# Moving the softmax denominators of a unit to one score bank, and the rows of their reciprocals to GpSimd

## The reference

```python
qkv = (tokens @ w_proj + b_proj).reshape(B, N, NUM_HEADS, 3 * HEAD_DIM)
q, k, v = jnp.split(qkv, 3, axis=-1)
attn = jnp.einsum('bihd,bjhd->bijh', q, k) * SCALE
attn = jax.nn.softmax(attn, axis=2)
res = jnp.einsum('bijh,bjhd->bihd', attn, v).reshape(B, N, NUM_HEADS * HEAD_DIM)
out = res @ w_out + b_out + tokens
```

## Time and profile before

| | before |
|---|---|
| median of 3 runs | 3090.85 us (3090.58 to 3091.7) |
| the profiled execution, its own time | 3092.63 us |
| its span in the profile | 3090.9 us |
| TensorE busy | 2674.5 us, 87% |
| VectorE busy | 2051.6 us, 66% |
| ScalarE busy | 1279.2 us, 41% |
| GpSimd busy | 635.7 us, 21% |
| granted TensorE clock, mean | 0.937 |

### The profile page before, as it was taken

One profiled execution on the slowest core, in us unless ns is written; L12 is line 12 of the kernel. 1 busy time (PEld: TensorE's weight loads), 2 busy tenths in 40 slices (PEclk: granted clock), 3 DMA queues, 4 the chain that ended last, 5 costly groups with the idle time before them and its releaser, 6 DMA issues.

```text
span 3090.9 us, 44860 instructions
## 1 busy us (share of the span) xinstructions
PE 2674.5 (87%) x15742; PEld 1889.2 (61%) x15742; DVE 2051.6 (66%) x2355; ACT 1279.2 (41%) x1860; POOL 635.7 (21%) x405
## 2 busy tenths in 40 slices
PE   6889979899798897988879888899888899888993
PEld 4457755577556775567755677457764477645772
DVE  4666667666676676666667566765677666766666
ACT  2553326433264333643336333463334533255334
POOL 0520116102160022500225002340024200252011
PEclk8999989999899998999999999999999999999996
DMA  6100050000500005000040001400022000410016
GB/s 150 32 25 1 1 130 2 25 1 14 117 1 25 1 14 117 2 24 1 21 110 1 24 1 36 95 12 14 1 66 66 25 1 1 95 37 25 1 55 245
DMA packets 46397, 124.71 MB, mean 40 GB/s; under 512 B 9792, under 2 KB 21312, under 8 KB 42560
## 3 DMA queue, kind: packets, MB, share of 16 engines
q1 hardware_dynamic: 46144, 121.41, 14.4%
HBM read 43.01 MB, written 23.86 MB: 22 GB/s over the span
## 4 chain that ended last, share of the span: by engine, by line
PE 74%; DVE 8%; issue 5%; ACT 5%; SPq 4%; DMA 3%; DVEq 0%; ACTq 0%
PE tile L1356 24%; PE pv L1356 10%; PE pv L1474 8%; PE tile L1436 7%; PE tile L1464 6%; PE tile L1623 4%; PE tile L1498 4%; SPq L522 3%; DMA stack<-qk_r 2%; PE pv L1464 2%; PE tile L1645 2%; PE tile L1753 1%; PE tile L1672 1%; PE tile L1523 1%; PE tile L1506 1%
## 5 line engine op out<-in xcount | busy, mean ns | idle before, releaser
L965 DVE TENSOR_REDUCE small<-tile 128x1 f32<-128x1024 f32 x512 | 599.1, 1218 | 169.8 <-PE tile L1436 169.8
L744 ACT ACTIVATE p<-tile 128x512 f32<-128x512 f32 (+1 forms) x640 | 410.2, 688 | 234.0 <-PE tile L1464 233.9
L1436 PE MATMUL tile<-stack 96*128 96x512 f32 x1024 | 348.8, 437 | 83.0 <-ACT stack L752 49.1
L1356 PE MATMUL tile<-qk_r 128*128 128x512 f32 x1536 | 377.9, 395 | 0.0
L653 POOL TENSOR_TENSOR row_sum<-act 128x256 f32<-128x256 f32 x32 | 42.1, 1334 | 1501.4 <-DVE act L1191 1501.4
L623 POOL TENSOR_TENSOR acc<-acc,p 128x1024 f32<-128x1024 f32 x144 | 339.4, 2385 | 0.0
L1436 PEld LDWEIGHTS tile<-stack 96*128 96x128 f32 x1024 | 177.8, 196 | 255.5 <-issue 118.1
L1356 PEld LDWEIGHTS tile<-qk_r 128*128 128x128 f32 x1536 | 287.1, 188 | 66.4 <-issue 7.7
L1196 DVE TENSOR_TENSOR pl<-p,ph 128x1024 fp32r<-128x1024 f32 x128 | 158.2, 1236 | 238.0 <-ACT p L838 238.0
L1464 PE MATMUL tile<-stack 112*128 112x512 f32 x768 | 271.2, 421 | 16.1 <-DVE rec L1013 9.2
L1474 PE MATMUL pv<-p,v 128*32 128x512 f32 x2048 | 271.8, 604 | 1.4 <-ACT p L744 1.4
(11 more groups left out here) (285 smaller groups left out, 4546.6 us busy)
## 6 DMA issues: line engine op xcount, KB each, us to landing
stack<-qk_r SPq DMA_DIRECT2D x192, 256.0 KB, 5.0
x_in<-in_x_dram SPq DMA_DIRECT2D x9, 1024.0 KB, 7.6
act<-in_x_dram SPq DMA_DIRECT2D x8, 1024.0 KB, 8.0
x_scratch<-act SPq DMA_DIRECT2D x7, 1024.0 KB, 3.9
z_scratch<-zbuf SPq DMA_DIRECT2D x7, 1024.0 KB, 5.3
stack<-ones SPq DMA_DIRECT2D x8, 512.0 KB, 7.6
w3f<-w3f_scratch SPq DMA_DIRECT2D x8, 512.0 KB, 3.3
fin_rest<-z_scratch SPq DMA_DIRECT2D x3, 1024.0 KB, 12.7
```

The lines of the kernel that those rows point to most:

```text
L744: sc.activation(p0[:, jt % DEPTH, pair, first:first + len(heads) * HALF], tile_wait(b, "st0", *u, jt, k), ACT.Exp, scale=float(D) ** -0.5) ...
L965: ve.tensor_reduce(maxima[:, h * NT + it:h * NT + it + 1], t[:], X, ALU.max).then_inc(vector_done, vector.one("max0", g, h, it))
L1356: ins = mm(out, lhs[a][kt_], rhs[c][kt_], start=first and kt_ == 0 and m == 0, stop=last and kt_ == n - 1 and m == 2)
L1436: ins = mm(o[:, s], stack[0:IMAX, 0, g, h, it * P:(it + 1) * P], stack[0:IMAX, 1, g, h, s], start=True, stop=True)
```

## The change

`den0` of the first three units leaves the ring "rows" for the ring "scores", as its 33rd entry in each unit, and reads and writes one bank. The order of that ring becomes first half of `tile2`, half of `pv`, second half of `tile2`. With 33 entries a unit, each `den0` then lands in the second half of `tile2`. The first `s0` of the next unit takes the tile that the last `s0` had, and the second one that of `m0`. The next unit's third `st0` takes the bank of `den0`. Ahead of the last unit the first `st0` takes a tile of `s0`, and the second one takes the whole of `tile2`, so it waits for `rec0`. `rows0` of the first three units is made by GpSimd, ahead of its `add0` of the next unit, and `ex0` waits for GpSimd. `rows0` of the last unit stays on VectorE.

```diff
@@ vector_steps
-            s += [("rec0", *last), ("rows0", *last)] if last and jt == 0 else []
+            s += [("rec0", *last)] if last and jt == 0 else []
@@ pool_steps
     for u in UNITS:
+        s += [("rows0", *last_unit(*u))] if last_unit(*u) else []
         for jt in range(1, summed(*u)):
@@ homes
-        ring = ("scores" if kind == "st0" else "rows") if looped else "whole"
+        ring = ("scores" if kind in ("st0", "den0") else "rows") if looped else "whole"
         if ring == "scores":
-            home[n] = ((2, 0), (2, 1), (3, 1 - n[2]))[rings[ring] % 3]
+            home[n] = ((2, 0), (3, 1 - n[2]), (2, 1))[rings[ring] % 3]
@@ GpSimd
                 for u in UNITS:
+                    if last_unit(*u):
+                        pool.wait_ge(vector_done, vector.at(b, "rec0", *last_unit(*u)))
+                        pe.tensor_tensor(rows0[:], rec0[:].rearrange("p (a n) -> p a n", a=1).broadcast_to((P, HT, P)),
+                                         seg_own[:].rearrange("p (t a) -> p t a", a=1).broadcast_to((P, HT, P)), ALU.mult
+                                         ).then_inc(pool_done, gps.one("rows0", *last_unit(*u)))
@@ VectorE
-                    return tile[slot(*name)]
+                    return where(*name)
@@ inverse0
                     ve.reciprocal(rec0[:], den[:, 0:P]).then_inc(vector_done, vector.one("rec0", *u))
+                    if next_unit(*u):
+                        return
                     own("rec0", *u)
@@ ex0
-                    vector_wait("rows0", g, half)
+                    if next_unit(g, half):
+                        pe.wait_ge(pool_done, gps.at(b, "rows0", g, half))
+                    else:
+                        vector_wait("rows0", g, half)
```

## The result

The changed kernel took 3067.07 us (median of four runs, 3064.62 to 3069.57) against 3091.27 us for the kernel before: 24.2 us or 0.8% less, ratio 0.992 (95% interval 0.9903 to 0.9937). A second set of five runs gave 3066.26 us, ratio 0.9914 (0.9901 to 0.9928). The forecast was 3072.4 us with a range down to 3067.6, so the kernel came out 0.5 us faster than the range allows (1.3 us in the second set). The profiled execution has a span of 3067.8 us, 23.1 us less than before. One of the four executions of `a_pad4`, further down, took 3530 us at a granted clock of 0.723, and its figures are those of the other three.

The account below looks back on a forecast made before the run. TensorE was taken to bound the kernel, with 74% of the chain of waits, standing still at 24 unit ends for the reciprocal. Gains of 10.9 + 7.5 = 18.4 us gave 3090.85 - 18.4 = 3072.4 us, range 3067.6 to 3080.

Parts of the forecast that it names:

- unit ends: Three places in each of eight images where score products wait for the denominators' reciprocal; forecast gain 18.4 us in all.
- inner end: Unit end inside the loop of units, 16 in all; second plain score 0.68 us earlier, 10.9 us in sum.
- last entry: Unit end before the last unit, 8 in all; product by the values 0.94 us earlier, 7.5 us in sum.
- What is late next: At inner ends, third transposed score, ScalarE's first exponential and VectorE's maxima must all move too, by 0.68 to 0.69 us.
- The third score: Third transposed score at an inner end, now in the denominators' bank; reciprocal done in time by 0.39 us.
- GpSimd's product: `rows0` at the three unit ends, taken as 1.3 us on GpSimd; even 2.7 us fits ahead of `ex0`, costing nothing.
- Rival 3: Inner ends: GpSimd's product holds VectorE's maxima, kernel 7.7 us slower, 3098.5 us; chance 0.03.
- rival 1: Only the inner ends give, 10.9 us, 3080 us; chance 0.10, shared with VectorE not moving the whole 0.69 us there.
- rival 4: Nothing to see: waits off the path, or the stop moves whole to the third score; 3091 us, chance 0.03.
- 10.9 + 7.5 = 18.4 us: Gains of the 16 inner ends and 8 last entries, taken off 3090.85 us to give 3072.4 us.
- what it gains at an end isn't taken back later in the unit: Loop between unit ends is TensorE's own, at granted clock 1.00 around the ends, so their gains were expected to stay.
- Rival 2: The whole reciprocal leaves the chain at all 24 unit ends, 23.3 us, 3067.6 us; chance 0.10.

Follow-up runs that it names:

- a_pad4: Changed kernel with four score products made twice in unit (0,1) of every image: median 3071.6 us, 5.3 us more than the changed kernel.
- e1_bank_only: Against the kernel before: denominators moved to the score bank as in the changed kernel, `rows0` left on VectorE; 3099.62 us, ratio 1.0016.
- clean images: Whole images at granted clock 1.00, both kernels with throwaway products in TensorE's waits: mean 368.58 us before the change, 366.37 us with it.
- b_pad8: Kernel before with eight score products made twice in unit (0,1) of every image: 1.8 us more, ratio 1.0008.
- a_pad10: Changed kernel with ten score products made twice in unit (0,1) of every image: ratio 0.9998 to the kernel before.

## Why the prediction was wrong, point by point

**The unit ends were read rightly.** An inner end was to give 0.68 us and gave 0.75; the last entry 0.94 and gave 0.98. In sum 16 x 0.75 + 8 x 0.98 = 19.8 us against 18.4. The forecast distance from the reciprocal's start to the first exponential was 1.34 us, and 1.33 were measured. The small excess has two sources in the rows. TensorE no longer waits 0.17 us for a maximum in `jt` 1, since the maxima start 0.72 us earlier and not 0.69. And at the last entry the second score starts 0.05 us behind the end of the reciprocal (554.76 against 554.71), where the prediction took over the start of before, 0.13 us behind it (557.31 against 557.18).

**"What is late next" held.** The third score didn't wait. It had 0.40 us to spare by the rows (493.86 against 493.46), and 0.39 was predicted. That the first part of the change is worth little without the second was put as a step, and `e1_bank_only` shows it: nothing at the inner ends, with VectorE's maxima holding both scores of `jt` 1. The two parts are worth 0.00 and 0.08 us alone, and 0.75 together.

**GpSimd's product** took 1.04 us, where 1.3 us was taken and 0.97 to 2.7 was the span of the rows. The nearest row was that of a broadcast product, halved (0.97), not that of the same shape. With 3.3 and 1.8 us left ahead of `ex0` it made no difference. What a longer one would cost was not tried. The Trainium skill, "GPSIMD Engine Reference", section "Elementwise — side-by-side cycle accounting", has GpSimd about twice as slow as VectorE in an addition of two tensors; here it was 1.04 against 0.69 us, 1.5 times. Maxima beside it took no longer, four in 4.55 us where it was 4.61. The Trainium skill, "SBUF — State Buffer", section "Who interferes with whom", says that such reductions never contend with GpSimd, and the trace agrees. Rival 3 is out. So are rival 1, by the last entry's 0.98 us, and rival 4, by all three distances.

**The step that failed** is the sum itself: "10.9 + 7.5 = 18.4 us", made against the whole execution as if the rest of the image stayed as it was. The forecast looked at the granted clock only around the ends, where it is 1.00, and concluded that "what it gains at an end isn't taken back later in the unit". That is true of the unit and says nothing of the image. The mean clock of 0.937 stood in the table of the kernel before, and nothing was made of it: the term for the clock was put at nothing. The runs showed that less of TensorE's work fell under the lower clock, 27.1 and 26.1 us of an image's rest in the two traces instead of 27.9, at about 0.5 us for each. The rest of the image was worth another 4 to 6 us here (24.2 and 26.3 us measured, less 19.8). By the clean images the change is worth 17.7 us, near the forecast's 18.4, and the kernel shows 24 to 26 us.

**The bounds were worked out wrongly for the same reason.** The lower end, 3067.6 us, was the whole of the reciprocal leaving the chain, the most that the ends could give. A term for the clock was missing on both sides. `b_pad8` shows how far it can go: 13 us of work for 1.8 us. `a_pad10` shows the other side: 16 us of work for 26 us. Rival 2, whose time the measurement nearly has, is not what happened: the reciprocal still holds the last entry's second score.

**What stays open.** That the lower clock is what the rests differ by is shown; why it falls where it does, and an image so settles at one length or another, is not. The kernel before, `b_pad8` and `a_pad10` all sit at 375.5 us an image, with 86.3 to 88.3 us of ends; the changed kernel sits at 372.1 in its second trace and at 372.6 in its first. `e1_bank_only` lies between them in its ends and doesn't settle (its images take 375.0 to 379.1 us, its runs 3083 to 3112 us). Which work makes a kernel fall on the one or the other side was not found.

## What to carry to other kernels

Two moves can each be worth nothing and together be worth the whole wait. So follow, for each engine, when its next instruction at the place would start, and move them all or none. In a loop whose TensorE falls to its lower clock in some of its waits, a small change of length may not be passed on one for one: judge it by the distances in the trace at the place that was changed, and put a term for the clock on both sides of the range. Where the granted clock is under 1 and waits are the reason, products that do nothing are worth a try before finer moves; here they gave more than the change.

## What the runs showed of the hardware

Where TensorE falls to its lower clock in some waits of a loop, the time need not follow the work. With 84.2, 86.3, 86.7 and 88.3 us of ends an image took 372.1, 375.5, 375.5 and 375.5 us; with 85.1 and 85.8 us it took 374.0 and 375.9 and didn't settle. Eight images absorbed 13 us of added TensorE work for 1.8 us. Half of the time in which TensorE was busy at the lower clock accounted for the differences of the rests in nine kernels to 0.3 us. Keeping TensorE busy through four of an image's waits raised the mean granted clock of the profiled execution from 0.937 to 0.962 in the kernel before and took 28 us off its time; filling the others raised it to 0.987 (0.982 to 0.984 in the other executions) and took off 15 more. A GpSimd product of two broadcast operands, 128 x 512, took 1.04 us, less than the 1.29 us of a subtraction of two plain tiles of that shape.
